# Transposed features of a recommendation tower stored feature by feature in place of row by row

## The chip, the cores and the metric

The kernel runs on one core of a Trainium2 chip. The metric is the device time of one execution in microseconds (us). The core has a matrix engine (TensorE, in the trace PE, its weight loads PEld), a vector engine (VectorE, DVE), a scalar engine (ScalarE, ACT), a general engine (GpSimd, POOL) and a queue engine (SyncE, SP). Each runs its own stream of instructions; semaphores order them. SBUF is the on-chip memory of 128 partitions, PSUM the accumulator that TensorE writes, in banks of 512 fp32 a partition.

## The reference

For each of 2048 rows, 27 embedding vectors of 128 numbers are looked up, all 351 products of two different ones are taken, and a three-layer network runs on the products and 16 dense inputs.

```python
e = jnp.stack([tbl_0[ids[:, 0]], ..., tbl_26[ids[:, 26]]], axis=1)      # (2048, 27, 128)
z = jnp.einsum('bfd,bgd->bfg', e, e)[:, _TRIL_I, _TRIL_J]               # 351 pairs, k=-1
h = jnp.concatenate([z, dense_ctx], axis=1)                             # (2048, 367)
h = jnp.maximum(h @ W_top1 + b_top1, 0.0)                               # 512
h = jnp.maximum(h @ W_top2 + b_top2, 0.0)                               # 256
y = h @ W_top3                                                          # (2048, 1)
```

All of it is fp32.

## The kernel before

The 2048 rows are 8 groups of 256 (`COLS`), a group being two tiles of 128. The program of an engine is a sequence of eight periods, one for each group: groups 0 and 1 are written out, groups 2 to 5 are two turns of a loop of two periods, groups 6 and 7 are written out again (on GpSimd the loop runs to the end).

Features come in two kinds. **Cold** features (18 or 19, by group) are gathered: GpSimd issues one indirect DMA for a tile and a feature (L390), which brings 128 embedding vectors into `rows`, one to a partition. TensorE transposes each of them with an identity matrix (L413), four features to a PSUM bank, five banks ("tile fills") for a tile. `rows` holds one copy of each tile, so GpSimd gathers tile 0 of the next group only when TensorE has transposed tile 0 of this one. **Hot** features (8 or 9, small tables) are looked up on TensorE: VectorE makes one-hot matrices from the ids (L635), and TensorE multiplies the tables, held in two parts, with them (L427, L429), two features to a PSUM bank ("hot fills"). In the first group ScalarE and VectorE also make the two parts of each table from the raw one (L532, L613) as it arrives.

Both kinds of fills go through a ring of four PSUM banks, `fill_ps` (`FILL_RING`). ScalarE copies each bank to `et`, the transposed features: 128 partitions (the embedding's dimension) times 256 rows times 27 features. L540 copies a tile fill (four features of 128 rows, the fifth less), L548 a hot fill (two features of 256 rows, the last one in some groups). TensorE fills a bank again when the copy of the fill four before has been counted in `fill_moved`.

Then TensorE takes, for each row, the product of its features with themselves (`row_pairs`, L488): a stationary operand of 26 features, a moving one of 26, for one row. An fp32 matmul is two instructions, so a bank of 64 rows is 128 matmuls and 128 weight loads. Four rows go to four 32-partition strips of one bank, and a group has four such banks (`pairs` 0 to 3; 0 and 1 read tile 0 alone), over two PSUM banks `pair_ps`. VectorE and ScalarE move two strips each to `work` (`move_pairs`, L328), small DMAs of SyncE complete the layout (L279), and the layers of the group before (L439, L465, L472; L453 and L512 in the last one) run between the banks. The order on TensorE is:

```python
start = (hot[:4] + [("tile", 0)] + hot[4:]
         + [("layer", 1), ("pairs", 0), ("layer", 2), ("tile", 1), ("pairs", 1)])
if last:
    return start + [("pairs", 2), ("pairs", 3), ("layer", 3)]
return start + [("layer", 3), ("pairs", 2), ("pairs", 3)]
```

with the first group's own: three hot fills, tile 0, the other hot fills, pairs 0 and 1, tile 1, pairs 2 and 3. ScalarE follows the same order with its copies and activations (L557, L563), in one queue.

Of the kernel before, what the change touches and what calls it, by code (L numbers as in the profile page):

```python
# [25 lines left out]
P = 128  # L26
BATCH = 2048
FEATURES = 27
# [24 lines left out]
COLS = GROUP_TILES * P  # L53
# [31 lines left out]
def fills(n_hot):  # L85
    return GROUP_TILES * N_TF + len(hot_fills(n_hot))
# [90 lines left out]
def wait_count(engine, semaphore, count):  # L177

    if not isinstance(count, int) or count > 0:
        engine.wait_ge(semaphore, count)  # L180


def build(nc, ids, ids_hot, tables, dense, w1, w2, vectors_dram, out):
    with ExitStack() as ctx:
        def sb(name, shape, dtype=F32):
            return ctx.enter_context(nc.sbuf_tensor(name, shape, dtype))
# [11 lines left out]
        first_row_int = sb("first_row_int", [P, 2], I32)  # L198
        first_row = sb("first_row", [P, 2])
        ident = sb("ident", [P, P])  # L200
        et = sb("et", [P, COLS, FEATURES])
        w1_sb = sb("w1_sb", [P, CHUNKS, HIDDEN1])
        w2_sb = sb("w2_sb", [P, K2, HIDDEN2])
        vectors = sb("vectors", [P, K2 + 2 * M2])
# [90 lines left out]
        def n_hot(turn, h):  # L295
            return (EARLY_HOT if isinstance(turn, int) and turn == 0 else LATE_HOT)[h]

        def before(turn, h, count):

            early, late = [count(n) for n in EARLY_HOT], [count(n) for n in LATE_HOT]  # L300
            if isinstance(turn, int) and turn == 0:
                return sum(early[:h])
            return turn * sum(late) + (sum(early) - sum(late) + sum(late[:h]))
# [97 lines left out]
        def _(pe):  # L401
# [74 lines left out]
            def row_pairs(turn, h, bank):  # L476

                i = 2 * turn + h

                all_moved = before(turn, h, fills) + fills(n_hot(turn, h))  # L480
                pe.wait_ge(fill_moved, all_moved - (N_TF if bank < TILE_BANKS else 0))

                wait_count(pe, pair_moved_v, i * PAIR_BANKS + bank - 1)
                wait_count(pe, pair_moved_a, i * PAIR_BANKS + bank - 1)
                for r in range(BANK_ROWS):
                    for s in range(STRIPS):
                        row = bank // TILE_BANKS * P + s * STRIP + bank % TILE_BANKS * BANK_ROWS + r
                        last = nc.tensor.matmul(  # L488
                            pair_ps[bank % 2][32 * s:32 * s + PAIR_COLS, r * PAIR_COLS:(r + 1) * PAIR_COLS],
                            et[:, row, 0:FEATURES - 1], et[:, row, 1:FEATURES], start=True, stop=True)  # L490
                last.then_inc(pair_full, 1)

            def period(turn, h):
# [25 lines left out]
        @block.scalar  # L519
        def _(act):  # L520
            load_hot_ids(act, 0, 0)

            def load_weights():
                act.wait_ge(lo_made, N_HOT)
                act.dma_start(w1_sb[:, :, :], w1.rearrange("(c p) n -> p c n", p=P)).then_inc(w_in, 16)
                act.dma_start(w2_sb[:, :, :], w2.rearrange("(c p) n -> p c n", p=P)).then_inc(w_in, 16)
                act.dma_start(vectors[:, :], vectors_dram).then_inc(w_in, 16)

            def make_high(k):

                act.wait_ge(raw_in[k % RAW_SLOTS], 16 * (k // RAW_SLOTS + 1))
                nc.scalar.copy(table_hi[0:HOT_ROWS, CHUNK_AT[k]:CHUNK_AT[k] + HOT_CHUNKS[k], :],  # L532
                               raw_table(k)).then_inc(hi_made, 1)

            def move_tile(turn, h, n0, t):

                for j, (c0, n) in enumerate(tile_fills(n_hot(turn, h))):

                    act.wait_ge(cold_full, (2 * turn + h) * (GROUP_TILES * N_TF) + t * N_TF + j + 1)
                    nc.scalar.copy(et[:, t * P:(t + 1) * P, c0:c0 + n].rearrange("p r f -> p f r"),  # L540
                                   fill_ps[(n0 + j) % FILL_RING][:, 0:n * P].rearrange("p (f r) -> p f r", f=n)
                                   ).then_inc(fill_moved, 1)

            def move_hot(turn, h, n0, j):
                k0, n = HOT_FILLS[j]
                slot = ORDER.index(HOT[k0])
                act.wait_ge(hot_used, before(turn, h, looked_up) + k0 + n)
                nc.scalar.copy(et[:, :, slot:slot + n].rearrange("p r f -> p f r"),  # L548
                               fill_ps[n0 % FILL_RING][:, 0:n * COLS].rearrange("p (f r) -> p f r", f=n)
                               ).then_inc(fill_moved, 1)  # L550

            def relu1(i):
                last = is_last(i)
                for m in range(K2):

                    act.wait_ge(h1_full, i * (K2 // 2) + (m if last else m // 2) + 1)
                    nc.scalar.activation(h1[:, m, :], fill_ps[m][:, 0:COLS] if last else mlp_psum(m), ACT.Relu,  # L557
                                         bias=b1_sb[:, m:m + 1]).then_inc(h1_done, 1)

            def relu2(i):  # L560
                for m in range(M2):
                    act.wait_ge(h2_full, i * M2 + m + 1)
                    nc.scalar.activation(h2[:, m, :], mlp_ps[m][:, 0:COLS], ACT.Relu,  # L563
                                         bias=b2_sb[:, m:m + 1]).then_inc(h2_done, 1)

            def period(turn, h):
                i = 2 * turn + h

                wait_count(act, hot_made, before(turn, h, looked_up))
                if not is_last(i):  # L570
                    load_hot_ids(act, i + 1, 1 - h)
                for (kind, j), n0 in steps(turn, h):
                    if kind == "hot":
                        if is_first(turn, h):
                            for k in range(2 * j + 3, min(2 * j + 5, N_HOT)):
                                make_high(k)
                        move_hot(turn, h, n0, j)
                        if is_first(turn, h) and j == N_HF - 1:
                            load_weights()
                    elif kind == "tile":  # L580
                        move_tile(turn, h, n0, j)
                    elif kind == "pairs":
                        if j == 0 and is_first(turn, h):
                            act.wait_ge(zt_clear, 1)
                        if j == 0:
                            wait_count(act, z_in, i * (16 * MOVES))
                        move_pairs(act, i, j, (2, 3), pair_moved_a, nc.scalar.copy)
                    elif j < 3:
                        (relu1, relu2)[j - 1](i - 1)
                if is_first(turn, h):  # L590
                    act.wait_ge(w_in, 16 * N_W)

            for k in range(3):
                make_high(k)
            periods(act, period)
            relu1(GROUPS - 1)
            relu2(GROUPS - 1)
# [123 lines left out]
```

## Time and profile before

| | |
|---|---|
| time, median of 3 runs | 451.23 us (447.68 to 451.83) |
| span of the profiled execution, first to last instruction | 448.7 us |
| TensorE busy (matmuls) | 344.4 us, 77% |
| GpSimd busy | 292.9 us, 65% |
| VectorE busy | 232.9 us, 52% |
| ScalarE busy | 211.2 us, 47% |
| granted clock of TensorE, mean | 0.928 |
| HBM read | 35.27 MB |

The profile gives the span of its execution, and no time of its own beside it; the median of the runs is 2.5 us above the span. A busy share counts the time in which an engine has an instruction under way. It averages stages with different limits: what a stage waits for is in the rows of waits and in the timeline.

### The profile page before, as it was taken

To read this page: it belongs to the slowest core of one execution; us is meant where nothing else is said; L and a number is where in the kernel's file an instruction comes from. 1 tells how busy PE (TensorE), PEld (TensorE's weight loads), DVE (VectorE), ACT (ScalarE), POOL (GpSimd) and SP (SyncE) were. 2 spreads that over 40 slices of the span, in tenths; PEclk is the share of its full clock that TensorE was granted. 3 is DMA by queue.
4 is the path that set the end of the run, shared out by engine and by line. 5 is a ranking of instruction groups with operands and counts; after the bars stand their busy time and mean duration, and the time that the engine had idled before them with its cause. 6 is when DMAs were issued, how large, how long until landed. Compare 5 with 4: busy or idle time off the path is not lost.

```text
span 448.7 us, 14258 instructions
## 1 busy us (share of the span) xinstructions
PE 344.4 (77%) x5982; PEld 309.6 (69%) x5982; DVE 232.9 (52%) x907; ACT 211.2 (47%) x431; POOL 292.9 (65%) x308
## 2 busy tenths in 40 slices
PE   0003563966999799979994999799979977899878
PEld 0003562856988598869883998698859966797755
DVE  0007567643945582669346682594548372770340
ACT  1110135355355726663566246836473556426832
POOL 3777600777737777777777777777777777777020
PEclk9999957766999999999998899999988996899989
DMA  3557431152732264237422731264226422222000
GB/s 92 166 160 139 153 131 53 48 172 62 98 85 54 57 101 116 53 66 110 100 52 66 118 90 53 57 103 113 54 57 95 122 54 54 58 60 54 13 10 4
DMA packets 23166, 37.06 MB, mean 83 GB/s; under 512 B 6285, under 2 KB 16893, under 8 KB 23106
## 3 DMA queue, kind: packets, MB, share of 16 engines
q0 software_dynamic: 9600, 19.33, 22.8%
q10 hardware_dynamic: 10112, 10.53, 8.2%
q1 hardware_dynamic: 3394, 6.30, 3.8%
q8 instruction: 49, 0.80, 0.8%
q14 instruction: 11, 0.09, 0.1%
HBM read 35.27 MB, written 0.01 MB: 79 GB/s over the span
## 4 chain that ended last, share of the span: by engine, by line
PE 58%; DMA 16%; ACT 12%; issue 9%; POOL 2%; DVE 2%; SPq 0%; ACTq 0%; DVEq 0%; POOLq 0%
PE fill_ps L427 17%; PE fill_ps L429 16%; PE pair_ps L488 10%; ACT et L540 9%; DMA hot_ids<-ids_hot_d 8%; PE mlp_ps L439 7%; DMA work<-tbl_d 7%; PE mlp_ps L465 6%; POOL rows L390 2%; PE fill_ps L413 2%; PE fill_ps L453 1%; ACT et L548 1%; ACT work L328 1%; DMA rows<-tbl_d,index 1%; DVE table_lo L613 1%
## 5 line engine op out<-in xcount | busy, mean ns | idle before, releaser
L390 POOL DMA_INDIRECT rows<-tbl_d,index x222 | 217.6, 980 | 73.6 <-issue 66.4
L427 PE MATMUL fill_ps<-one_hot,table_hi 125*128 125x256 f32 x610 | 162.6, 303 | 56.7 <-DVE table_lo L613 40.9
L427 PEld LDWEIGHTS fill_ps<-one_hot,table_hi 125*128 125x128 f32 x610 | 128.0, 210 | 59.0 <-issue 56.5
L429 PE MATMUL fill_ps<-one_hot,table_lo 125*128 125x256 f32 x610 | 160.0, 299 | 0.0
L635 DVE TENSOR_SCALAR one_hot<-hot_ids 125x256 fp32r<-125x256 f32 x610 | 137.9, 301 | 14.3 <-PE fill_ps L429 13.4
L429 PEld LDWEIGHTS fill_ps<-one_hot,table_lo 125*128 125x128 f32 x610 | 128.0, 210 | 0.0
L328 DVE COPY work<-pair_ps 26x112 f32<-26x112 f32 (+1 forms) x256 | 66.0, 258 | 100.0 <-PE pair_ps L488 96.9
L390 POOL DMA_INDIRECT rows<-tbl_d,ids_sb x72 | 71.4, 991 | 51.4 <-PE fill_ps L413 24.4
L548 ACT COPY et<-fill_ps 128x512 f32<-128x512 f32 (+1 forms) x37 | 42.4, 1147 | 96.5 <-PE fill_ps L429 93.3
L540 ACT COPY et<-fill_ps 128x512 f32<-128x512 f32 (+2 forms) x80 | 78.5, 1175 | 4.6 <-PE fill_ps L413 4.6
L488 PE MATMUL pair_ps<-et 128*26 128x26 f32 x4096 | 56.4, 197 | 30.8 <-issue 18.1
L488 PEld LDWEIGHTS pair_ps<-et 128*26 128x26 f32 x4096 | 47.4, 109 | 44.3 <-issue 34.4
L328 ACT COPY work<-pair_ps 26x112 f32<-26x112 f32 (+1 forms) x256 | 60.9, 238 | 34.8 <-PE pair_ps L488 32.0
L413 PE MATMUL fill_ps<-ident,rows 128*128 128x128 f32 x294 | 44.0, 299 | 13.5 <-ACT et L548 6.9
L413 PEld LDWEIGHTS fill_ps<-ident,rows 128*128 128x128 f32 x294 | 36.1, 153 | 19.8 <-ACT et L548 8.7
L623 DVE TENSOR_SCALAR hot_ids<-hot_ids,first_row 125x1280 f32<-125x1280 int32 (+1 forms) x16 | 12.7, 836 | 65.7 <-DMA hot_ids<-ids_hot_d 65.7
L439 PE MATMUL mlp_ps<-work,w_sb 128*128 128x256 f32 x168 | 37.5, 380 | 0.0
L439 PEld LDWEIGHTS mlp_ps<-work,w_sb 128*128 128x128 f32 x168 | 31.4, 190 | 4.1
L532 ACT CAST table_hi<-work 125x1024 fp32r<-125x1024 f32 (+1 forms) x7 | 7.9, 1135 | 52.4 <-DMA work<-tbl_d 52.4
L465 PE MATMUL mlp_ps<-work,w_sb 128*128 128x256 f32 x128 | 29.7, 385 | 0.0
L465 PEld LDWEIGHTS mlp_ps<-work,w_sb 128*128 128x128 f32 x128 | 23.8, 190 | 3.2
L557 ACT ACTIVATE work<-mlp_ps,vectors 128x256 f32<-128x256 f32 x28 | 11.7, 471 | 19.1 <-PE mlp_ps L439 19.1
(24 smaller groups left out, 63.4 us busy)
## 6 DMA issues: line engine op xcount, KB each, us to landing
hot_ids<-ids_hot_d ACTq DMA_DIRECT2D x8, 1125.0 KB
rows<-tbl_d,index POOLq DMA_INDIRECT x222
work<-tbl_d SPq DMA_DIRECT2D x4, 500.0 KB
work<-tbl_d SPq DMA_DIRECT2D x3, 625.0 KB
rows<-tbl_d,ids_sb POOLq DMA_INDIRECT x72
w_sb<-w_d ACTq DMA_DIRECT2D x1, 768.0 KB, 4.8
w_sb<-tbl_d SPq DMA_DIRECT2D x1, 625.0 KB
w_sb<-w_d ACTq DMA_DIRECT2D x1, 512.0 KB, 5.7
```

Of the source, the lines that this page charges most:

```text
L328: last = copy(pair_cols[STRIP * q:STRIP * q + PAIR_COLS, place(q + 1)[1]:, at:at + BANK_ROWS], frm[:, q::STRIPS, :])
L390: nc.gpsimd.indirect_dma_start(out=rows[:, t, c, :], out_offset=None, in_=tables[f], in_offset=bass.IndirectOffsetOnAxis(ap=numbers[:, f:f ...
L413: last = nc.tensor.transpose(bank[:, c * P:(c + 1) * P], rows[:, t, c0 + c, :], ident[:, :])
L427: nc.tensor.matmul(to, table_hi[0:HOT_ROWS, CHUNK_AT[k] + c, :], hot, start=(c == 0), stop=False)
L429: last = nc.tensor.matmul(to, table_lo[0:HOT_ROWS, CHUNK_AT[k] + c, :], hot, start=False, stop=(c == HOT_CHUNKS[k] - 1))
L439: last = nc.tensor.matmul(mlp_psum(m), w1_sb[:, c, m * P:(m + 1) * P], zt[:, c, :], start=(c == 0), stop=(c == CHUNKS - 1))
L465: last = nc.tensor.matmul(mlp_ps[m][:, 0:COLS], w2_sb[:, c, m * P:(m + 1) * P], h1[:, c, :], start=(c == 0), stop=(c == K2 - 1))
L488: last = nc.tensor.matmul(pair_ps[bank % 2][32 * s:32 * s + PAIR_COLS, r * PAIR_COLS:(r + 1) * PAIR_COLS], et[:, row, 0:FEATURES - 1], et[ ...
L540: nc.scalar.copy(et[:, t * P:(t + 1) * P, c0:c0 + n].rearrange("p r f -> p f r"), fill_ps[(n0 + j) % FILL_RING][:, 0:n * P].rearrange("p ( ...
L548: nc.scalar.copy(et[:, :, slot:slot + n].rearrange("p r f -> p f r"), fill_ps[n0 % FILL_RING][:, 0:n * COLS].rearrange("p (f r) -> p f r", ...
L623: nc.vector.tensor_scalar(ids.bitcast(F32), ids, first_row[0:HOT_ROWS, n:n + 1], None, ALU.subtract).then_inc(hot_ids_local, 1)
L635: last = nc.vector.tensor_scalar(one_hot[0:HOT_ROWS, k % HOT_RING, c, :], hot_ids[0:HOT_ROWS, h, k, :].bitcast(F32), float(c), None, ALU.i ...
```

## The change

`et` keeps its size and its contents. Its last two dimensions change places: a partition held 256 rows of 27 features, and now holds 27 features of 256 rows. ScalarE's copies write runs of 128 or 256 neighbouring elements, where they wrote elements 27 apart; TensorE's row products read 26 columns that lie 256 elements apart, where they read 26 neighbouring ones. The number, the order and the waits of the instructions are the same on all engines.

```diff
-        et = sb("et", [P, COLS, FEATURES])
+        et = sb("et", [P, FEATURES, COLS])
...
                         last = nc.tensor.matmul(
                             pair_ps[bank % 2][32 * s:32 * s + PAIR_COLS, r * PAIR_COLS:(r + 1) * PAIR_COLS],
-                            et[:, row, 0:FEATURES - 1], et[:, row, 1:FEATURES], start=True, stop=True)
+                            et[:, 0:FEATURES - 1, row], et[:, 1:FEATURES, row], start=True, stop=True)
...
-                    nc.scalar.copy(et[:, t * P:(t + 1) * P, c0:c0 + n].rearrange("p r f -> p f r"),
+                    nc.scalar.copy(et[:, c0:c0 + n, t * P:(t + 1) * P],
                                    fill_ps[(n0 + j) % FILL_RING][:, 0:n * P].rearrange("p (f r) -> p f r", f=n)
                                    ).then_inc(fill_moved, 1)
...
-                nc.scalar.copy(et[:, :, slot:slot + n].rearrange("p r f -> p f r"),
+                nc.scalar.copy(et[:, slot:slot + n, :],
                                fill_ps[n0 % FILL_RING][:, 0:n * COLS].rearrange("p (f r) -> p f r", f=n)
                                ).then_inc(fill_moved, 1)
```

## Rows read from the trace of the kernel before

**Rows 1.** The page, part 1: busy us (share of the span) and instructions
```profile
PE 344.4 (77%) x5982; PEld 309.6 (69%) x5982; DVE 232.9 (52%) x907; ACT 211.2 (47%) x431; POOL 292.9 (65%) x308
```

**Rows 2.** The page, part 4: the chain that ended last, by line
```profile
PE fill_ps L427 17%; PE fill_ps L429 16%; PE pair_ps L488 10%; ACT et L540 9%; DMA hot_ids<-ids_hot_d 8%; PE mlp_ps L439 7%; DMA work<-tbl_d 7%; PE mlp_ps L465 6%; POOL rows L390 2%; PE fill_ps L413 2%; PE fill_ps L453 1%; ACT et L548 1%; ACT work L328 1%; DMA rows<-tbl_d,index 1%; DVE table_lo L613 1%
```

**Rows 3.** GpSimd's waits (us, times, longest) and its share of 130.6:415.6 (busy, clock, DMA)
```profile
POOL rows L390 <- issue: 87.8, 288, 0.3
POOL rows L390 <- PE fill_ps L413: 31.5, 5, 24.4
...
130.60:415.60 285.00, 217.60 (x222) 0.95 0.35 76
```

**Rows 4.** Timeline of GpSimd: start, us, instruction, [idle before <-releaser]
```profile
130.63 0.94 POOL L390 DMA_INDIRECT rows<-tbl_d,index  x1 [6.24 <-PE fill_ps L413]
```

**Rows 5.** Timeline, GpSimd and TensorE, around the second tiles of groups 6 and 7
```profile
368.98 0.94 POOL L390 DMA_INDIRECT rows<-tbl_d,index  x1 [0.30 <-issue]
371.56 4.31 PE L413 MATMUL fill_ps<-ident,rows 128*128 128x128 f32 x19 [3.97 <-DMA rows<-tbl_d,index]
...
414.65 0.94 POOL L390 DMA_INDIRECT rows<-tbl_d,index  x1 [0.30 <-issue]
...
419.47 2.32 PE L413 MATMUL fill_ps<-ident,rows 128*128 128x128 f32 x18
```

**Rows 6.** Groups of ScalarE by line and form: count | busy us, mean ns | idle before
```profile
L540 ACT COPY et<-fill_ps 128x512 f32<-128x512 f32 x64 | 68.7, 1255 | 4.6 <-PE fill_ps L413 4.6
L548 ACT COPY et<-fill_ps 128x512 f32<-128x512 f32 x32 | 39.1, 1222 | 94.7 <-PE fill_ps L429 91.7 <-DVE one_hot L635 3.0
L557 ACT ACTIVATE work<-mlp_ps,vectors 128x256 f32<-128x256 f32 x28 | 11.7, 471 | 19.1 <-PE mlp_ps L439 19.1
L540 ACT COPY et<-fill_ps 128x256 f32<-128x256 f32 x10 | 7.7, 769 | 0.0
L532 ACT CAST table_hi<-work 125x1024 fp32r<-125x1024 f32 x4 | 4.2, 1044 | 41.7 <-DMA work<-tbl_d 41.7
L532 ACT CAST table_hi<-work 125x1280 fp32r<-125x1280 f32 x3 | 3.8, 1257 | 10.7 <-DMA work<-tbl_d 10.7
```

**Rows 7.** The chain in order of time (start, us, what), first group and tile 0 of group 1
```profile
74.91 1.07 ACT et L548
75.97 2.06 ACT et L540 x2
...
98.85 4.71 ACT et L540 x5
...
127.07 1.20 ACT et L548
```

**Rows 8.** Timeline of TensorE, group 2's tile 0 and the third bank of products
```profile
173.37 2.11 PE L413 MATMUL fill_ps<-ident,rows 128*128 128x128 f32 x16
175.85 0.55 PE L413 MATMUL fill_ps<-ident,rows 128*128 128x128 f32 x3 [0.36 <-ACT et L540]
...
192.84 0.57 PE L488 MATMUL pair_ps<-et 128*26 128x26 f32 x46 [0.84 <-ACT et L540]
```

**Rows 9.** Timeline of the last group, ScalarE and TensorE
```profile
420.11 4.75 ACT L540 COPY et<-fill_ps 128x512 f32<-128x512 f32 x5
...
424.91 1.61 PE L488 MATMUL pair_ps<-et 128*26 128x26 f32 x128 [1.92 <-ACT et L540]
```

**Rows 10.** L488: its group, and banks in three windows: us, matmuls, loads, clock, DMA
```profile
L488 PE MATMUL pair_ps<-et 128*26 128x26 f32 x4096 | 56.4, 197 | 30.8 <-issue 18.1 <-ACT et L540 8.4 <-ACT et L548 0.8
...
107.43:109.17 1.74, 1.74 (x108) 1.53 (x108) 0.50 0.19 47
138.14:139.96 1.82, 1.71 (x128) 1.38 (x128) 1.00 0.15 45
421.72:422.99 1.27, 1.27 (x128) 1.16 (x128) 1.00 0.00 0
```

**Rows 11.** The chain in order of time: layer 1 of one period
```profile
221.58 5.18 PE mlp_ps L439 x24
```

## The prediction

> **What bounds the kernel now.** I read the busy shares first. No engine is above 77% [rows 1], so the shares name no bound and the waits have to. In the chain of waits most lines are TensorE's, from 17% down; ScalarE's copies of L540 hold 9% of the span and those of L548 1% [rows 2]. The copies of L540 and L548 are the ones that the change rewrites; L488, the row products, is where it changes what TensorE reads.
>
> Second view: GpSimd. It issues the cold look-ups one after the other. Of its idle time before them, 87.8 us are 0.30 us pieces between two gathers and only 31.5 us are waits for TensorE [rows 3]. From 130.6 us to the last one at 415.6 us it issues 222 gathers in 285.0 us, 1.284 us each, with no gap but those pieces [rows 3, 4]. It had ended the gathers of the group before at 124.4 us; the 6.24 us of idle time up to 130.63 were ended by TensorE's transposes of group 1 [rows 4]. So there are two chains. TensorE's chain runs through all groups. GpSimd's chain starts at 130.6 us, when tile 0 of group 1 has been transposed, lasts 285 us whatever TensorE does, and is followed by the tail of the last group. They touch twice: in group 6 TensorE waited 3.97 us for rows, which came 1.6 us after the gather that began at 368.98 and took 0.94 had ended, and in group 7 it began the last tile at 419.47, when the rows (last gather 414.65 + 0.94, and 1.6 to land) were there at 417.2 [rows 5]. TensorE is the later one by 2.3 us. What TensorE alone saves in the middle of the program is therefore lost; what is saved before 130.6 us, in the last group and in the tail counts.
>
> **The change part by part.** *ScalarE's copies.* They read PSUM as before; the place of neighbouring elements in SBUF changes from 108 bytes apart (27 features of 4 bytes) to next to each other. Before, a 128x512 copy took 1255 ns on L540 and 1222 ns on L548; one of 256 took 769 [rows 6]. For packed writes the nearest rows are the ScalarE activation from PSUM, 128x256 in 471 ns, and the casts of 1024 and 1280 elements in 1044 and 1257 ns, a slope of 213/256 = 0.83 ns an element [rows 6]. So 512 packed elements take 471 + 256 x 0.83 = 684 ns, 256 take 471. The saving in busy time is 64 x 0.571 + 32 x 0.538 + 10 x 0.298 = 36.5 + 17.2 + 3.0 = 56.7 us of ScalarE's 211, and some 3 us more for eleven smaller copies at 0.2 to 0.4 us each. Its other bound is nothing at all, if the time sits in the reading of PSUM. Against that stands that the activation reads the same PSUM without it; I take the full saving.
>
> Most of this only makes ScalarE's idle time longer: it is waited for only where the ring of four fill banks or the row products need a copy. Place by place:
> First group, tile 0: the chain goes table cast, L548 1.07 us, two copies L540 2.06 us, then TensorE [rows 7]. Three copies at 0.69 us in place of 3.13: 1.1 us. The one-feature copy at the group's end: 0.2 us.
> First group, tile 1: ScalarE starts five copies at 98.85 and ends them 4.70 us later; TensorE's next products wait for them [rows 7]. Now 4 x 0.69 + 0.47 = 3.2 us: 1.5 us.
> Group 1, tile 0: a hot copy from 127.07 in 1.20 us [rows 7], then two tile copies as in the first group, 2.06, so TensorE goes on at 130.33. Now 127.07 + 3 x 0.69 = 129.14: 1.2 us for TensorE. The tile's last two transposes, which release GpSimd, ended about 0.5 us before that, at 129.8, and now end at about 128.9, since the bank they wait for comes free at 127.07 + 2 x 0.69 = 128.45: 0.9 us.
> Every later tile 0: 1.2 us in groups 3, 5, 7 by the same order, 0.5 us in groups 2, 4, 6, where layer 1 follows without a fifth hot fill and 19 transposes took from 173.37 to 176.40, 3.03 us, for 19 x 2.11/16 = 2.5 us of work [rows 8]. With group 1: 4 x 1.2 + 3 x 0.5 = 6.3 us.
> Waits before the third bank of row products: 0.84 us in group 3's period [rows 8], five such waits from 0.58 to 0.89, 3.7 us together, gone because five copies take 3.2 us in place of 4.7 to 5.1 and TensorE has 1.8 us of products and 0.8 us of layer 3 before it.
> Tail: five copies from 420.11 in 4.75 us, for which TensorE waits 1.92 us [rows 9]. Now they end at 423.4, when TensorE has ended the second bank at 423.0 [rows 10]: 1.5 us. What is late next there is ScalarE's own move of that bank, which starts as the copies end (424.86 before, 423.4 now), so the 1.5 us stay.
>
> *The row products.* Both operands of each product, 26 columns, were packed and are now 1024 bytes apart from column to column. 4096 matmuls and 4096 weight loads read so. No row of the trace shows TensorE reading anything but packed columns, so this cost has to be bounded from outside. What the rows give: a bank of 128 matmuls takes 1.82 us at a granted clock of 1.00 (2.4 GHz); less the 0.20 us of the last one that is (1.82 - 0.20)/127 = 12.8 ns from one to the next. At 0.50 (1.2 GHz) 108 of them took 1.74 us, 14.4 ns; and one bank in the tail ran in 1.27 us, 8.4 ns each [rows 10]. Halving the clock changes the pace by an eighth, so in most banks the array is not what limits it. The pauses before L488 put down to "issue", 18.1 us in all [rows 10], in which no semaphore is missing, point to the supply of instructions. Four products run side by side in four 32-column strips, so a strip has 4 x 12.8 = 51 ns for each of its matmuls, and the whole stay of one is 197 ns.
> Lower bound: nothing. A gain is excluded, since the pace does not hang on the reading today. Upper bounds, from the nearest row with far-apart elements, ScalarE's writes: the slope from 256 to 512 elements on L540 is (1255 - 769)/256 = 1.90 ns, say 1.9 [rows 6]; 26 x 1.9 = 49 ns an operand. (a) The strips read side by side and the weight load lies behind the matmul before: 49 ns in a strip's 51, nothing changes. (b) Load and matmul in line, or two passes over the elements: 99 ns, 24.7 ns a matmul, 1.5 us more a bank. (c) The strips share one path: 49 ns a matmul, (49 - 12.8) x 128 = 4.6 us more a bank. I take (a), since a strip's time is enough for it and the four strips demonstrably run at the same time; I hold it with less than even chance because it has 2 ns to spare.
>
> The Trainium skill, "Advanced Engine Details and Errata", section "SBUF Cachelines", speaks against this change: it says that SBUF is reached in lines of 16 bytes and that going to a different line with each element costs. ScalarE's rows agree for writes, 1.90 against 0.83 ns an element [rows 6]; for TensorE no row shows it, and the page gives no size. The Trainium skill's "Vector Engine (DVE) Microarchitecture Reference", section "Measured stream behaviour on trn2", has one source that hops with each element at 1.73 ns a column against 1.054 packed; an estimate by that figure would be 45 ns an operand, so (a) no change, (b) 22.5 ns a matmul, 1.2 us more a bank, which in B's sum below would be 38 us in place of 48. As mechanisms of this kernel such dearer reads are the rivals B and C.
>
> *Sum.* GpSimd's chain starts earlier by 1.1 + 0.2 + 1.5 + 0.9 = 3.7 us (it could use 5.9 at most, since its group 1 ends at 124.7 with its last piece of 0.30). In group 7 the rows are then there at 413.5. TensorE comes from group 6, where the rows released it 3.7 us earlier, saves 1.2 in tile 0 of group 7 and is there at 419.47 - 4.9 = 414.6; still the later, but now by 1.1. Tail 1.5. Span: 448.7 - 4.9 - 1.5 = 442.3 us. The span lies 2.5 us below the median of the three runs, 451.23, and I keep that distance: **444.8 us**, 1.4% faster. TensorE's own chain without its wait for rows would be 448.7 - 4.0 - (2.8 + 6.3 + 3.7 + 1.5) = 430.4 us, so it has 12 us of cover.
>
> **The rivals.** With d us more a bank of products there are 32 banks. GpSimd's chain grows by 7 d (four banks before its start, three behind the last tile): 442.3 + 7 d. TensorE's grows by 32 d less what the pauses give back, at most 18.1 us: 430.4 + 32 d.
> *A, the forecast:* d = 0 or below 0.3. 442.3 to 444.4 in the span, 444.8 to 447 as a time.
> *Even:* d between 0.4 and 0.9, or the copies do not get shorter as the change says because PSUM's side sets them. Time 447 to 456, 451 in the middle. For it: a reading cost that is there but fits mostly in the slack. Chance 0.13.
> *B, slower, load and matmul in line in each strip:* d = 1.5. TensorE becomes the bound in each group: 430.4 + 48.0 = 478.4, less 0 to 18.1 of pauses, 460.3 to 478.4; middle 469.4, and with the 2.5 a time of 472. GpSimd then waits for TensorE in every group. It decides against the change from d = 0.8 (no pause given back) or 1.3 (all). For it: four strips and the weight path all read at the same time. Against: a transpose, a load of 128 columns with a product of 128, takes 132 ns (16 in 2.11, with small waits) [rows 8], and the same load with an fp32 product of 256 comes every 216 ns (24 in 5.18) [rows 11]; that speaks for a load that lies behind the product, at least for whole-array ones. Chance 0.25.
> *C, the strips share one path to SBUF:* d = 4.6. 430.4 + 147.2 = 577.6, less up to 18.1: 559.5 to 577.6, time about 571. For it: ScalarE's one stream already takes 1.9 ns an element when its elements lie far apart, and here eight such streams, four of products and four of loads, would be open at once. Against: they are open at once today, at 8.4 ns a matmul [rows 10]. Chance 0.18.
>
> **How the numbers follow.** A 0.44, even 0.13, B 0.25, C 0.18. The measurement of this kernel can tell about 1%, 4.5 us, from no change (the three runs spread over 4.2 us). Faster by over 1% is A, 0.44; within 1% is the even case, 0.13; slower is B and C, 0.43. The predicted time is A's, 444.8. The range leaves out C, 0.18, and little below: from 441 (A, and 4 us below it, as far as the runs of one kernel spread) to 483 (B with no pause given back, 481, and its d of 1.5 uncertain). A alone has 441 to 448.
>
> **What would show it.** In the profile after: L540 and L548 128x512 near 0.69 us, ScalarE busy near 151 us. A bank of L488 still at 1.3 to 1.8 us with 128 matmuls; if the matmul's own 197 ns grow while the pace stays, that is (a). GpSimd's last gather near 412 us, its waits for TensorE at two places only. B would show 3.3 us a bank, no "issue" pauses before L488, and GpSimd waiting before each tile 0; C 6.4 us a bank. The prediction is wrong if the products' pace follows the reads, or if the copies stay near 1.2 us.

## Result and profile after

The changed kernel took **473.11 us** (median of 4 runs, 471.57 to 475.8) beside 450.87 us for the kernel before: 1.052 times the time, 95% interval 1.047 to 1.058. The forecast was 444.8 us; the time lies on the other side of no change. It is close to the 472 us of rival B, but B is not what happened, as the rows show.

The page of the changed kernel, part 1 (compare [rows 1]), and part 4, the chain that ended last, by engine and by line (compare [rows 2]):

```profile
PE 379.6 (81%) x5982; PEld 358.1 (76%) x5982; DVE 266.4 (57%) x907; ACT 203.6 (43%) x431; POOL 320.5 (68%) x308
...
POOL 51%; issue 16%; DMA 15%; PE 11%; DVE 3%; ACT 2%; SPq 1%; POOLq 0%; DVEq 0%
POOL rows L390 51%; DMA hot_ids<-ids_hot_d 8%; DMA work<-tbl_d 7%; PE pair_ps L488 3%; PE fill_ps L427 3%; PE fill_ps L429 3%; DVE work L328 2%; SPq L279 1%; PE fill_ps L413 1%; PE mlp_ps L465 1%; DMA rows<-tbl_d,index 1%; DVE table_lo L613 1%; ACT et L540 0%; ACT table_hi L532 0%; PE fill_ps L453 0%
```

The chain has moved to GpSimd. TensorE is busy for 35 us more and holds only 11% of it. The groups by line and form (count | busy us, mean ns | idle before), beside [rows 6] and [rows 10]:

```profile
L488 PE MATMUL pair_ps<-et 128*26 128x26 f32 x4096 | 104.0, 285 | 5.1 <-issue 2.7 <-ACT et L540 1.5 <-ACT et L548 0.5
L390 POOL DMA_INDIRECT rows<-tbl_d,index x222 | 240.4, 1083 | 67.7 <-issue 67.7
L540 ACT COPY et<-fill_ps 128x512 f32<-128x512 f32 x64 | 48.1, 845 | 20.2 <-PE fill_ps L413 20.2
L548 ACT COPY et<-fill_ps 128x512 f32<-128x512 f32 x32 | 18.7, 586 | 103.8 <-PE fill_ps L429 100.6 <-issue 3.2
L557 ACT ACTIVATE work<-mlp_ps,vectors 128x256 f32<-128x256 f32 x28 | 28.3, 1237 | 31.9 <-PE mlp_ps L439 31.9
L642 DVE COPY y_row<-mlp_ps 1x256 f32<-1x256 f32 x8 | 11.2, 1398 | 14.7 <-PE mlp_ps L472 14.4
```

The same lines of the kernel before:

```profile
L390 POOL DMA_INDIRECT rows<-tbl_d,index x222 | 217.6, 980 | 73.6 <-issue 66.4 <-PE fill_ps L413 7.1
L642 DVE COPY y_row<-mlp_ps 1x256 f32<-1x256 f32 x8 | 3.3, 412 | 14.6 <-PE mlp_ps L472 14.3
```

ScalarE's copies got shorter as forecast where they run alone: 586 ns on L548, from 1222. But L557, an activation that the change doesn't touch, went from 471 to 1237 ns, and the copy of L642 from 412 to 1398. Neither reads or writes `et`. The timeline of the changed kernel around the first bank of products of group 1 (start, us, instruction) shows when:

```profile
131.72 5.69 DVE L635 TENSOR_SCALAR one_hot<-hot_ids 125x256 fp32r<-125x256 f32 x14
...
132.52 5.01 POOL L390 DMA_INDIRECT rows<-tbl_d,index  x1 [0.30 <-issue]
...
133.23 3.21 PE L488 MATMUL pair_ps<-et 128*26 128x26 f32 x128
133.34 3.20 ACT L557 ACTIVATE work<-mlp_ps,vectors 128x256 f32<-128x256 f32 x2 [1.75 <-PE mlp_ps L439]
```

A bank takes 3.21 us (1.82 before, [rows 10]). Two activations that need 0.84 us together lie under it from its beginning to its end, and a gather that meets it takes 5.01 us in place of 0.94. That gather does not end with the bank: the bank ends at 136.44 and the gather at 137.53. What ends 0.12 us before the gather is VectorE's unbroken row of 14 one-hot instructions (131.72 + 5.69 = 137.41), within which it had begun. The bank had stretched that row; one instruction of L635, 282 ns in the median, takes up to 3161 ns in this trace. The same in the table of GpSimd's line (min/median/max ns), with the longest gathers from the chain in order of time:

```profile
L390 POOL DMA_INDIRECT rows<-tbl_d,index x222: 940/947/5150, 129.9 to 436.8; - x111
L390 POOL DMA_INDIRECT rows<-tbl_d,ids_sb x72: 940/947/4342, 7.5 to 128.5; - x72
...
132.52 5.01 POOL rows L390
178.72 3.98 POOL rows L390
227.38 3.35 POOL rows L390
295.04 2.91 POOL rows L390
328.09 3.85 POOL rows L390
377.41 5.15 POOL rows L390
```

The median gather is as it was, 947 ns. Seven are not: these six and the one of 4342 ns in group 1, 28.6 us together; at 0.98 us each they would be 6.9, so being held cost **21.7 us**. The other gathers are a little longer too. In all GpSimd is busy for 320.5 - 292.9 = 27.6 us more. The span grew by less, 470.9 - 448.7 = 22.2 us, because the shorter copies gave some 5 us back: e5 below, the new layout with packed reads, has a span of 443.6 us and GpSimd busy for 293.0, and from there to the changed kernel the span grows by 27.3 us and GpSimd's busy time by 27.5. No gather of the kernel before lasted over 1.51 us. Each of the seven ends 0.12 us after an instruction of VectorE has ended, and none at the end of a bank. GpSimd's waits confirm that it sets the end:

```profile
POOL rows L390 <- issue: 88.7, 291, 0.3
POOL rows L390 <- PE fill_ps L413: 25.1, 2, 24.8
PE fill_ps L413 <- DMA rows<-tbl_d,index: 17.2, 5, 6.8
```

Beside one wait of 24.8 us at the start it waits for TensorE for 0.3 us in the whole program (before, 31.5 us in five waits, of which one was 24.4, [rows 3]), and TensorE waits five times for rows.

### The profile page after: what moved, and what is told of

Same layout as the page of the kernel before. It is cut to its first block, busy times and chain, and to the rows that moved or that the text cites. A ratio compares the mean times of both kernels' runs of the same rounds, so it can differ in the third digit from the quotient of the medians.

```text
span 470.9 us, 14258 instructions
## 1 busy us (share of the span) xinstructions
PE 379.6 (81%) x5982; PEld 358.1 (76%) x5982; DVE 266.4 (57%) x907; ACT 203.6 (43%) x431; POOL 320.5 (68%) x308
## 4 chain that ended last, share of the span: by engine, by line
POOL 51%; issue 16%; DMA 15%; PE 11%; DVE 3%; ACT 2%; SPq 1%; POOLq 0%; DVEq 0%
POOL rows L390 51%; DMA hot_ids<-ids_hot_d 8%; DMA work<-tbl_d 7%; PE pair_ps L488 3%; PE fill_ps L427 3%; PE fill_ps L429 3%; DVE work L328 2%; SPq L279 1%; PE fill_ps L413 1%; PE mlp_ps L465 1%; DMA rows<-tbl_d,index 1%; DVE table_lo L613 1%; ACT et L540 0%; ACT table_hi L532 0%; PE fill_ps L453 0%
## 5 line engine op out<-in xcount | busy, mean ns | idle before, releaser
L390 POOL DMA_INDIRECT rows<-tbl_d,index x222 | 240.4, 1083 | 67.7 <-issue 67.7
L427 PE MATMUL fill_ps<-one_hot,table_hi 125*128 125x256 f32 x610 | 157.4, 297 | 54.5 <-DVE table_lo L613 41.3
L427 PEld LDWEIGHTS fill_ps<-one_hot,table_hi 125*128 125x128 f32 x610 | 123.9, 203 | 55.5 <-issue 55.2
L635 DVE TENSOR_SCALAR one_hot<-hot_ids 125x256 fp32r<-125x256 f32 x610 | 152.4, 339 | 7.4 <-PE fill_ps L429 6.8
L328 DVE COPY work<-pair_ps 26x112 f32<-26x112 f32 (+1 forms) x256 | 80.1, 313 | 93.1 <-PE pair_ps L488 89.7
L488 PEld LDWEIGHTS pair_ps<-et 128*26 128x26 f32 x4096 | 100.4, 211 | 10.7 <-issue 7.0
L488 PE MATMUL pair_ps<-et 128*26 128x26 f32 x4096 | 104.0, 285 | 5.1 <-issue 2.7
L328 ACT COPY work<-pair_ps 26x112 f32<-26x112 f32 (+1 forms) x256 | 79.0, 309 | 17.2 <-PE pair_ps L488 13.6
L548 ACT COPY et<-fill_ps 128x512 f32<-128x512 f32 (+1 forms) x37 | 20.6, 557 | 111.9 <-PE fill_ps L429 108.7
L540 ACT COPY et<-fill_ps 128x512 f32<-128x512 f32 (+2 forms) x80 | 56.0, 842 | 20.2 <-PE fill_ps L413 20.2
L413 PE MATMUL fill_ps<-ident,rows 128*128 128x128 f32 x294 | 40.5, 299 | 22.7 <-DMA rows<-tbl_d,index 17.2
L557 ACT ACTIVATE work<-mlp_ps,vectors 128x256 f32<-128x256 f32 x28 | 28.3, 1237 | 31.9 <-PE mlp_ps L439 31.9
```

What stands on the lines that cost most here:

```text
L328: last = copy(pair_cols[STRIP * q:STRIP * q + PAIR_COLS, place(q + 1)[1]:, at:at + BANK_ROWS], frm[:, q::STRIPS, :])
L390: nc.gpsimd.indirect_dma_start(out=rows[:, t, c, :], out_offset=None, in_=tables[f], in_offset=bass.IndirectOffsetOnAxis(ap=numbers[:, f:f ...
L413: last = nc.tensor.transpose(bank[:, c * P:(c + 1) * P], rows[:, t, c0 + c, :], ident[:, :])
L427: nc.tensor.matmul(to, table_hi[0:HOT_ROWS, CHUNK_AT[k] + c, :], hot, start=(c == 0), stop=False)
L488: last = nc.tensor.matmul(pair_ps[bank % 2][32 * s:32 * s + PAIR_COLS, r * PAIR_COLS:(r + 1) * PAIR_COLS], et[:, 0:FEATURES - 1, row], et[ ...
L540: nc.scalar.copy(et[:, c0:c0 + n, t * P:(t + 1) * P], fill_ps[(n0 + j) % FILL_RING][:, 0:n * P].rearrange("p (f r) -> p f r", f=n)).then_i ...
```

## Experiments

The kernels were timed in five series, each on one chip and with the kernel before between the others; a ratio is to that. e1 to e5, e7 to e9, e12 and e15 take other elements of `et` for the row products, so those are products of other numbers; the others leave nothing out.

### A series in which TensorE stood still with no semaphore missing

Four kernels; the edits of e2, e3 and e4 are shown with e7, e8 and e9, which are the same files. The edit for packed operands, 26 neighbouring elements of one feature inside the row's own tile:

```diff
+                        f, at = row % FEATURES, row // P * P + row * 7 % 102
...
-                            et[:, 0:FEATURES - 1, row], et[:, 1:FEATURES, row], start=True, stop=True)
+                            et[:, f, at:at + 26], et[:, f, at + 1:at + 27], start=True, stop=True)
```

> The changed kernel, but both operands of each row product are 26 neighbouring elements of one feature (so the products are of other numbers; all else is the change). In the changed run the banks of products took 3.2 us and GpSimd's gathers 1.08 us. Theory S (far-apart reads of TensorE hold up every other engine's use of SBUF, and through GpSimd's gathers the whole): with packed reads banks at 1.8 us, gathers back at 0.98 us, the activation of L557 back from 1237 to 471 ns, time 441 to 447 us. Rival T (only TensorE's own pace makes the time; the other engines' longer instructions are a by-product of the new layout's writes): banks 1.8 us and a time near 445 us too, but gathers and activations stay long.

> As the kernel with both operands packed, and before each bank of products seven fp32 matmuls of the identity with itself, 128 columns, into the same PSUM bank (14 instructions at 109 ns, 1.5 us): TensorE is held as long a bank as in the changed kernel, about 3.3 us, with no far-apart read. Theory S: gathers stay at 0.98 us, TensorE's chain of 454 us in the span or GpSimd's of 453 sets the end, time 453 to 460 us, well below the changed kernel's 473. Rival T: the time follows TensorE's pace alone, 470 to 475 us.

> Only the moving operand is read as in the change, 1024 bytes from column to column; the stationary one is packed (products of other numbers). If the moving side is the one that costs: bank near 3.2 us, gathers near 1.08, time near 473. If both sides cost in line (the prediction's rival B): bank near 2.5 us, time between 448 and 465. If only the weight load costs: bank 1.8 us, time near 445.

> The mirror of the one before: only the stationary operand is read 1024 bytes from column to column. If the weight load is the one that costs: bank near 3.2 us, time near 473. If both in line: bank near 2.5 us. If only the moving side costs: bank 1.8 us, time near 445. Which of the two makes the other engines' instructions long shows in L557 (471 or over 1200 ns).

The kernel before took 737.97 us here. Measured: e1 728.67 (ratio 0.982, 0.973 to 0.991), e2 767.15 (1.040), e3 727.76 (0.986), e4 733.32 (0.992). The waits of e1:

```profile
PEld pair_ps L489 <- issue: 292.9, 291, 4.7
POOL rows L390 <- PE fill_ps L413: 282.4, 14, 33.8
PE pair_ps L489 <- issue: 260.5, 259, 4.5
```

TensorE stands before its products 259 times, about 1 us each, with no semaphore missing; in e3, with one far-apart operand, 252 times. I read it as instructions that come too slowly; the traces show only that nothing else is missing. GpSimd then waits 282 us for it. These times say nothing on the theories; only stretches without a pause could. The same four kernels are e5, e7, e8 and e9 below.

### The copies alone, and the copies' order of writing

> The changed kernel with both operands of each row product packed (26 neighbouring elements of one feature, so products of other numbers), once more: the four runs before lay at 728 to 767 us with the kernel before at 738, and TensorE stood still for some 0.7 us every few products there, with or without far-apart reads. If the kernel before is again near 451 us: theory S (far-apart reads of TensorE hold up every other engine's use of SBUF) gives banks of products at 1.8 us, gathers at 0.98 us, L557 at 471 ns, time 441 to 447 us. Rival T (only TensorE's own pace counts) gives the same time but gathers and activations as long as in the changed run (1.08 us and 1237 ns).

> The kernel before with its own layout (a row's 27 features side by side); ScalarE's copies run over rows outside and features inside, so that each writes 4 (or 2) neighbouring elements and then goes on 108 bytes further, and reads PSUM 128 (or 256) elements apart in place. Nothing is left out. TensorE's reads stay packed. Theory: what makes the copies long is a write that goes to another place with every element; then 128x512 copies take 0.6 to 0.8 us on L540 (runs of four) and 0.6 to 0.9 on L548 (runs of two), TensorE and GpSimd as before, time 442 to 447 us. Rival: reading PSUM far apart costs ScalarE as much, copies stay at 1.2 us or more, time 449 to 455 us.

The edit of e6, on the kernel before (L548 likewise):

```diff
-                    nc.scalar.copy(et[:, t * P:(t + 1) * P, c0:c0 + n].rearrange("p r f -> p f r"),
-                                   fill_ps[(n0 + j) % FILL_RING][:, 0:n * P].rearrange("p (f r) -> p f r", f=n)
+                    nc.scalar.copy(et[:, t * P:(t + 1) * P, c0:c0 + n],
+                                   fill_ps[(n0 + j) % FILL_RING][:, 0:n * P].rearrange("p (f r) -> p r f", f=n)
```

e5: 443.97 us beside 449.08, ratio 0.990 (0.986 to 0.994). e6: 445.72, ratio 0.993 (0.989 to 0.996). The groups of e5, then those of e6:

```profile
L390 POOL DMA_INDIRECT rows<-tbl_d,index x222 | 217.7, 981 | 67.7 <-issue 67.4 <-PE fill_ps L413 0.3
L541 ACT COPY et<-fill_ps 128x512 f32<-128x512 f32 x64 | 33.6, 603 | 11.2 <-PE fill_ps L413 11.1
L558 ACT ACTIVATE work<-mlp_ps,vectors 128x256 f32<-128x256 f32 x28 | 11.8, 471 | 29.0 <-PE mlp_ps L439 29.0
```

```profile
L540 ACT COPY et<-fill_ps 128x512 f32<-128x512 f32 x64 | 37.0, 676 | 9.4 <-PE fill_ps L413 9.4
L548 ACT COPY et<-fill_ps 128x512 f32<-128x512 f32 x32 | 26.1, 814 | 103.1 <-PE fill_ps L429 97.4 <-issue 3.0 <-DVE one_hot L635 2.7
```

With packed reads the packed writes give what was forecast of them, and gathers and activations are back, with no gather over 1.51 us: it was TensorE's reading that made them long, not the new layout's writes (rival T's second half falls). e6 shows that ScalarE reads PSUM 512 or 1024 bytes apart at little cost: what costs is a write that goes elsewhere with each element. Runs of four neighbours bring 1255 down to 676 ns, runs of two 1222 to 814.

### TensorE's pace or its reads; one side or both; one word more

> Both operands packed (products of other numbers), and before each bank of products seven fp32 matmuls of the identity with itself, 128 columns, into the same PSUM bank: 14 instructions at 109 ns, 1.5 us, so TensorE is held about as long a bank as by the far-apart reads, with none of them. Theory S (far-apart reads of TensorE hold up the other engines, and GpSimd's slowed gathers set the end): gathers stay at 0.98 us, time 453 to 460 us (TensorE's chain with 48 us more less 18 of pauses, 460 in the span, or GpSimd's 453). Rival T (TensorE's pace alone): 470 to 475 us, as in the changed kernel.

> Only the moving operand is read 1024 bytes from column to column; the stationary one is packed (products of other numbers). If the moving side is the one that costs: bank near 3.2 us, L557 over 1200 ns, gathers near 1.08 us, time near 473. If both sides add up (the prediction's rival B): bank 2.3 to 2.6 us, time 448 to 462. If only the weight load costs: bank 1.8 us, time near 444.

> The mirror of it: only the stationary operand is read 1024 bytes from column to column. If the weight load is the one that costs: bank near 3.2 us, L557 over 1200 ns, time near 473. If both sides add up: bank 2.3 to 2.6 us. If only the moving side costs: bank 1.8 us, time near 444.

> The changed kernel with nothing left out, and one element more between two features: 1028 bytes from column to column in place of 1024. Theory P (columns a power of two apart fall on the same part of the memory, and their order is the cost): bank back to 1.8 to 2.2 us, other engines' instructions back, time 443 to 450. Theory S in its plain form (any read that goes elsewhere with each element costs): bank 3.2 us, gathers 1.08 us, time 470 to 476.

```diff
# e7, on the packed kernel
+                for _ in range(7):
+                    nc.tensor.matmul(pair_ps[bank % 2][:, 0:P], ident[:, :], ident[:, :], start=True, stop=True)
# e8
-                            et[:, 0:FEATURES - 1, row], et[:, 1:FEATURES, row], start=True, stop=True)
+                            et[:, f, at:at + 26], et[:, 1:FEATURES, row], start=True, stop=True)
# e9
+                            et[:, 0:FEATURES - 1, row], et[:, f, at + 1:at + 27], start=True, stop=True)
# e10, on the changed kernel
-        et = sb("et", [P, FEATURES, COLS])
+        et = sb("et", [P, FEATURES, COLS + 1])
```

The kernel before: 449.67 us. e7 464.43 (ratio 1.036, 1.028 to 1.044), e8 446.35 (0.995, 0.991 to 0.999), e9 448.25 (0.999, 0.995 to 1.003), e10 **444.55** (0.989, 0.986 to 0.993). One unbroken bank of each of e8, e9 and e10, from their timelines, one fence each, with e10's gathers and activations under the bank:

```profile
130.61 2.14 PE L489 MATMUL pair_ps<-et 128*26 128x26 f32 x128
```

```profile
131.27 2.18 PE L489 MATMUL pair_ps<-et 128*26 128x26 f32 x128
```

```profile
129.93 1.75 POOL L390 DMA_INDIRECT rows<-tbl_d,index  x1 [0.30 <-issue]
...
130.43 2.00 PE L488 MATMUL pair_ps<-et 128*26 128x26 f32 x128
130.54 0.88 ACT L557 ACTIVATE work<-mlp_ps,vectors 128x256 f32<-128x256 f32 x2 [1.75 <-PE mlp_ps L439]
```

e7: TensorE spends 57.0 us on the added matmuls and 53.3 on the products, 110 us, more than the 104 of the changed kernel. Its look-ups on TensorE (L427) run at the changed kernel's pace, 295 against 297 ns, so no faster clock helps it. Gathers stay at 988 ns, GpSimd waits for TensorE seven times (35.0 us), and TensorE holds 69% of the chain; yet the kernel is 9 us ahead of the changed one (the intervals 1.028 to 1.044 and 1.047 to 1.058 don't meet). It missed the 453 to 460 of theory S by 4 us, TensorE's added matmuls taking 57.0 us where I had counted 48; rival T, 470 to 475, falls.

One gather of e7 was held all the same, with no bank of products near it, and again beside VectorE's one-hot instructions; it began within this row and ended 0.8 us after its end:

```profile
276.73 2.51 DVE L638 TENSOR_SCALAR one_hot<-hot_ids 125x256 fp32r<-125x256 f32 x12
...
277.42 2.63 POOL L390 DMA_INDIRECT rows<-tbl_d,index  x1 [3.79 <-PE fill_ps L413]
```

e8 and e9: one far-apart operand makes a bank 2.1 to 2.2 us, whichever it is, and costs the others little on average (L557, there L558, 485 ns in both, gathers 995 and 1000). But three gathers of e8 took 2.4 us and two of e9 3.0, each until 0.12 us after an instruction of VectorE had ended. The first of e8, beside VectorE:

```profile
129.50 2.83 DVE L636 TENSOR_SCALAR one_hot<-hot_ids 125x256 fp32r<-125x256 f32 x13
130.09 2.37 POOL L390 DMA_INDIRECT rows<-tbl_d,index  x1 [0.30 <-issue]
```

So a gather can be held behind VectorE's row of one-hot instructions under any reads of TensorE. What the two far-apart operands add is that the row itself lasts some 3 us longer. I take this from the times in the traces; no run moves the one-hot instructions away from the banks.

Each expectation had a middle way, both sides adding up with 2.3 to 2.6 us a bank; it comes nearest, but a side alone is cheaper than that, and the two together, 3.21 us, stretch the instructions of ScalarE and VectorE, which neither does alone.

e10 is the surprise: the same 26 columns on as many different places, both operands, 1028 bytes apart in place of 1024, and a bank is back at 2.0 us, the two activations under it at 0.88 us. The gather of 1.75 us above is its longest. Far-apart reading in itself is cheap for TensorE; both operands with columns exactly 1024 bytes apart are not.

### Where the operands meet

> The changed kernel with nothing left out and four elements more between two features: 1040 bytes from column to column. One element more had brought a bank of products from 3.24 to about 2.05 us. If what counts is that the columns of an operand move through the low part of the address, a step of 16 bytes does it at least as well as one of 4: bank 1.8 to 2.1 us, L557 at 471 ns, time 442 to 447. If what counts is that columns no longer stand at the same place within a piece of 16 bytes, four elements more bring nothing: bank 3.2 us, time near 473.

> The changed kernel, 1024 bytes from column to column on both sides, but the moving operand is taken 16 rows (64 bytes) further on, so that stationary and moving columns never share the low part of their addresses (products of other numbers). If it is the meeting of the two operands that costs (each alone far apart cost 2.2 us a bank, both 3.24): bank near 2.1 us, time near 446. If one place serves all columns that lie 1024 bytes apart, whatever their offset: bank 3.2 us, time near 473.

> The kernel before with ScalarE's loops swapped, as in the run at 445.7, and a row's features 28 elements apart in place of 27, so that each run of four begins on a 16-byte boundary. Nothing is left out. If the boundary matters to writes: the 128x512 copies of L540 fall from 676 to about 600 ns and those of L548 from 814 to about 650; if not, they stay. The end is set by GpSimd's gathers and TensorE's banks as before, so the time is 443 to 446 us either way.

> The same with nine hot features in every group (late groups had 8 and 9). GpSimd issues 6 gathers fewer (3 groups of two tiles, 1.284 us each, 7.7 us), TensorE looks up one more feature of 10 chunks in three groups (3 x 20 matmuls at 0.12 us, 7.2 us) and does 6 transposes and fills less (0.7 us). If GpSimd's chain sets the end when copies are short: 438 to 442 us. If TensorE's does: 446 to 451 us.

```diff
# e11: COLS + 4.  e12 and e15, on the changed kernel:
+                        other = row // P * P + (row + 16) % P
-                            et[:, 0:FEATURES - 1, row], et[:, 1:FEATURES, row], start=True, stop=True)
+                            et[:, 0:FEATURES - 1, row], et[:, 1:FEATURES, other], start=True, stop=True)
# e13, on e6: et of [P, COLS, FEATURES + 1].  e14, besides: LATE_HOT = (9, 9)
```

The kernel before was at 738.86 us in this series, too: e11 731.0 (0.990), e12 731.74 (0.990), e13 730.25 (0.989), e14 706.6 (0.955, 0.951 to 0.959). The whole times don't answer the questions asked of them, e14's neither, which e16 asks again of the padded kernel. The last period's banks, which came in one piece, do; e11, then e12:

```profile
693.37 1.92 PE L488 MATMUL pair_ps<-et 128*26 128x26 f32 x128
```

```profile
694.11 2.13 PE L489 MATMUL pair_ps<-et 128*26 128x26 f32 x128
```

With 1040 bytes a bank takes 1.92 us; with 1024 bytes, but the moving operand 64 bytes further on, 2.13. (The rows go round within the tile, so the last 16 of each have the moving operand 448 bytes back in place of 64 on.) In e13, where each run of four starts on a 16-byte boundary, the copies of L540 fell from 676 to 612 ns, while those of L548 rose from 814 to 883, for which I have no reason. I had expected both to fall.

> Again the changed kernel with the moving operand taken 16 rows (64 bytes) further on than the stationary one (products of other numbers). In the stretches without a pause the run before went at 15.0 ns a matmul, against 23.6 where both operands have the same low part of the address. If the meeting of the operands is the cost in an undisturbed run too: bank 2.1 to 2.2 us, L557 near 490 ns, gathers 0.98 to 1.00 us, time 444 to 449. Otherwise bank 3.2 us, 473.

> One element more between two features, and nine hot features in every group, nothing left out: 6 gathers fewer (7.7 us of GpSimd), 60 look-up matmuls more on TensorE (7.2 us). From 444.6: if GpSimd's chain sets the end, 437 to 441 us; if TensorE's does, 445 to 452 us.

> The changed kernel as it is, with nine hot features in every group. It tells what sets the end of the changed kernel. If GpSimd's gathers do (1.386 us each there, 307.8 us for 222 of them): 6 fewer give 8.3 us, 463 to 468 us. If TensorE does, as rival B of the prediction had it: 7.2 us of look-ups more, 474 to 481 us.

The kernel before: 450.18 us. e15: 450.06 (1.000, 0.997 to 1.004), its banks 2.12 to 2.23 us, L557 499 ns, gathers 990 on average. The pace came out as expected; the time lies 1 us above the expected 444 to 449, and 5 us above e10's. In its profiled execution, 447.93 us, two gathers were held for 2.40 and 1.81 us, and GpSimd is busy for 295.2 us against 293.3 in e10; that covers about 2 of the 5 us, the rest has no cause that I know. So with both operands 1024 bytes a column, their offset against each other decides: 3.21 us a bank when it is a multiple of 1024 bytes, 2.2 when 64 bytes more.

e17: 470.19 us (1.044, 1.035 to 1.052), between both theories. TensorE as the only bound, 474 to 481, is out; in the chain GpSimd has 36% and TensorE 31%. But the forecast of 463 to 468 was too good; its gathers:

```profile
L390 POOL DMA_INDIRECT rows<-tbl_d,index x216 | 240.1, 1111 | 65.8 <-issue 65.2 <-PE fill_ps L413 0.6
...
L390 POOL DMA_INDIRECT rows<-tbl_d,index x216: 941/952/6312, 130.3 to 435.0; - x108
```

216 gathers take 240.1 us, as 222 did (240.4). What GpSimd loses hangs on the banks that it runs into, not on the number of gathers: seven were held again, for 3.7 to 6.31 us.

e16: **437.95 us** (0.974, 0.967 to 0.981), nothing left out, faster than both kernels. One word of padding keeps the short copies, and the moved feature takes some 7.7 us from GpSimd, by the estimate made before. The time is what was expected if GpSimd set the end, 437 to 441. Yet its chain is TensorE's again, so the agreement doesn't show that GpSimd sets it:

```profile
PE 68%; DMA 17%; issue 6%; SPq 4%; DVE 2%; ACT 2%; DVEq 0%
...
L390 POOL DMA_INDIRECT rows<-tbl_d,index x216 | 211.5, 979 | 66.1 <-issue 64.9 <-PE fill_ps L413 1.2
```

## Why the prediction was wrong

**The step that failed** is in *The row products*: "I take (a), since a strip's time is enough for it". Going from bound to value, it priced only TensorE's own stream. It then held at once for TensorE and for all others. Two things were off.

1. *The size.* The pace in place of 12.8 ns was (3.21 - 0.29)/127 = 23.0 ns a matmul, 1.4 us more a bank, against 0 forecast and 1.5 in rival B. The reason given for B, load and matmul in line at ScalarE's price of an element, is not borne out: in e10, e11 and e15 both operands are as far apart and a bank takes 1.9 to 2.2 us. What costs is two operands whose columns are 1024 bytes apart and which have the same offset within 1024 bytes. B's 24.7 ns a matmul lies near the 23.0 measured, and its 472 us near the 473.11, by luck: it asks for the same price of 1028 bytes, where the bank took 2.00 us.

2. *The path.* Neither (a), (b) nor (c), nor any rival, had other engines in it. The sum took "1.284 us whatever TensorE does" for GpSimd's gathers. That was true of packed reads. Under the far-apart ones TensorE's banks stretched VectorE's and ScalarE's instructions, and seven gathers of 294 were held for 2.9 to 5.2 us, each until VectorE had ended an instruction. GpSimd's busy time grew by 27.5 us over e5's, 21.7 of them in these seven, and the span by 27.3. GpSimd was the very engine that the prediction had found to set the end. With the bank's 1.4 us more, the prediction's own formula for GpSimd's chain, 442.3 + 7 d, would give 452.1 in the span; 470.9 was measured. B's 472 us came from TensorE's chain (430.4 + 48 less pauses); in the run TensorE waited 17.2 us for rows, and e7, with TensorE held as long and no far-apart read, took 464.4.

**What held.** *GpSimd as the second chain*: e5 ends its last gather at 408.97 + 0.94 = 409.9 us, 5.7 before the kernel before (forecast 3.7), and starts group 2 at 124.83, at once after group 1, so the start used all it could. *The copies*: forecast 684 ns, measured 603 and 586; ScalarE's busy time in e5 fell to 152.0 us (forecast 151). *The time with packed reads*, 444.8 forecast, 443.97 in e5 and 444.55 in e10. That it is so close is partly luck: as a gain over the kernel before it is 5.1 us, against 6.4 forecast, and the kernel before was faster there, 449.08. *The tail* didn't give its 1.5 us. TensorE in the tail of e5:

```profile
413.17 2.13 PE L413 MATMUL fill_ps<-ident,rows 128*128 128x128 f32 x18
415.23 2.02 PE L489 MATMUL pair_ps<-et 128*26 128x26 f32 x213
419.70 1.37 PE L489 MATMUL pair_ps<-et 128*26 128x26 f32 x128 [2.45 <-issue]
423.80 0.71 PE L489 MATMUL pair_ps<-et 128*26 128x26 f32 x42 [2.73 <-issue]
```

The wait of 1.92 us for ScalarE ([rows 9]) is gone, and pauses of 2.45 and 2.73 us stand in its place; as I read it, TensorE, with nothing to wait for, runs into the end of its instructions earlier. From the start of the last transposes to the end it is 443.6 - 413.2 = 30.4 us, against 29.2 before. What GpSimd's start gave beyond the forecast made up for most of it.

**Lines of 16 bytes.** The Trainium skill, "Advanced Engine Details and Errata", section "SBUF Cachelines", says that a different line with each access costs. For ScalarE's writes the runs agree in degree: 1255 ns at one element a place, 676 in runs of four, 603 packed. For TensorE's reads they agree weakly: packed 1.82 us a bank, 1.9 to 2.2 with each column on another line. They don't explain the change: 1024 and 1028 bytes are the same by that rule and differ by 3.21 to 2.00 us.

**Open.** Which bits of the address make the meeting, and whether it is the load and the matmul of one strip or of different strips that meet (the strips' rows lie 128 bytes apart in all these kernels), wasn't tried. Nor why VectorE and ScalarE, which read and write elsewhere, are held by such a bank. Why only seven gathers were caught is open as well: six of them met the first bank of a group, beside VectorE's one-hot instructions, and the seventh one of VectorE's moves, but of the gathers that began within the same instructions elsewhere nine in ten took 0.94 to 1.07 us. Some 3 us of e15 are unexplained.

## What to carry to other kernels

Before both operands of a TensorE product are laid out with one large stride, look at where their columns fall. Here 1024 bytes, the only power of two that was tried, with the same offset on both sides was the bad case, and one element of padding turned 5.2% slower into 1.1% faster. When one engine's access pattern is changed, price it for every engine that runs beside it, above all for the one that sets the end; instructions that a change doesn't touch and that grow in the profile after are the sign. See then where a lengthened instruction ends: here that pointed from GpSimd to VectorE, and not to TensorE. A scattered write can gain much by the order of the loops alone, so that it goes in short runs: here 1255 ns became 676.

## What the hardware showed that I had not expected

- Two TensorE operands, both with columns 1024 bytes apart at the same offset, slow its products from 12.8 to 23.0 ns and hold ScalarE and VectorE: an activation of 471 ns took 3080 at most, a one-hot instruction of 282 up to 3161. Either operand alone, or both with 1028 or 1040 bytes or 64 bytes of offset, gives 1.9 to 2.2 us a bank and leaves those instructions nearly as they were.
- A gather of GpSimd that begins within VectorE's row of one-hot instructions can be held: 5.01 us in place of 0.94 in the changed kernel, up to 6.31 in e17, 2.4 in e8, and with packed reads 2.63 in e7. In the changed kernel all seven ended 0.12 us after an instruction of VectorE.
- ScalarE writes elements 108 bytes apart at 2.1 times the packed duration (1255 against 603 ns for 128x512); runs of four cost 676 ns, and its reads of PSUM 512 bytes apart show next to nothing.
- In two of five series the same kernel before took 738 us in place of 450. In the traces of e1 and e3, from one of them, TensorE stood about 1 us before its products 259 and 252 times without a missing semaphore.
